# Slot one-hots by 32 f16 tensor-scalar operations that carry the token number

## The reference, cut to what matters

```python
x = x + xattn(layernorm(x), ctx_1024, ...)        # 2 x 1024 tokens of 256, 16 heads, 64 keys
xf = layernorm(x).reshape(2048, 256)
scores = softmax(xf @ gate_w.T)                   # 8 experts
_, sel = top_k(scores + expert_bias, 2)           # 2 experts of each token
order = argsort(sel.reshape(-1), stable=True)     # (token, choice) pairs sorted by expert
token_idx = order // 2
routed = xf[token_idx] * top_scores_sorted
routed_out = grouped_ffn(routed, w1, w2, w3, counts)   # h = silu(x w1[e]) * (x w3[e]); h w2[e]
out = zeros.at[token_idx].add(routed_out)
x = x + out
```

## Time and profile before

| | us |
|---|---|
| three timed runs | 415.96, 419.43, 426.19 (median 419.43) |
| the profiled execution | 411.13 |
| its span, first to last instruction | 409.4 |
| attention and loads (about) | 0 to 149 |
| routing after the prefix matmuls | 149 to 162 |
| experts and the copy out | 162 to 409 |
| busy: TensorE, DVE, ACT, POOL | 358.7, 239.3, 197.4, 234.8 |

### The profile page before, as it was taken

One profiled execution on the slowest core, in us unless ns is written; L12 is line 12 of the kernel. 1 busy time (PEld: TensorE's weight loads), 2 busy tenths in 40 slices (PEclk: granted clock), 3 DMA queues, 4 the chain that ended last, 5 costly groups with the idle time before them and its releaser, 6 DMA issues.

```text
span 409.4 us, 10006 instructions
## 1 busy us (share of the span) xinstructions
PE 358.7 (88%) x2668; PEld 263.6 (64%) x2669; DVE 239.3 (58%) x615; ACT 197.4 (48%) x343; POOL 234.8 (57%) x288
## 2 busy tenths in 40 slices
PE   2767999999999894889999999999999999999810
PEld 2546888888787552457667776677777677776510
DVE  1887767777673578275555555656555656555400
ACT  4577989889887420243343443343443343443200
POOL 7448978887788801224546655556656556663330
PEclk9896999999999996999999999999999999999985
DMA  7944979978977010357677777777777778888636
GB/s 226 355 77 113 254 201 240 243 214 217 253 226 239 31 20 2 78 124 128 130 129 132 138 141 138 129 136 127 143 141 138 128 137 128 142 139 125 98 37 215
DMA packets 121524, 61.55 MB, mean 150 GB/s; under 512 B 97170, under 2 KB 116124, under 8 KB 121468
## 3 DMA queue, kind: packets, MB, share of 16 engines
q1 hardware_dynamic: 113408, 50.45, 51.6%
q0 software_dynamic: 7488, 10.39, 17.2%
q10 hardware_dynamic: 604, 0.41, 0.6%
HBM read 28.88 MB, written 11.60 MB: 99 GB/s over the span
## 4 chain that ended last, share of the span: by engine, by line
PE 74%; DVE 8%; DMA 6%; issue 4%; ACT 3%; POOL 2%; POOLq 0%; SPq 0%; ACTq 0%; DVEq 0%
PE sc L1419 12%; PE sc L1421 11%; PE sc L1420 11%; PE bank L1307 7%; PE bank L1435 6%; PE bank L1438 6%; PE bank L1437 5%; PE bank L1355 3%; PE ptps L1369 3%; DMA acc<-xn,put_now 3%; DMA w_hi<-n_L_xattn_in_proj_weight 2%; PE bank L1322 2%; POOL w_lo L516 1%; PE sc L1244 1%; PE sc L1275 1%
## 5 line engine op out<-in xcount | busy, mean ns | idle before, releaser
L608 POOL DMA_INDIRECT acc<-xn,put_now x39 | 62.3, 1597 | 74.3 <-DVE xn L1149 68.5
L1419 PE MATMUL sc<-w_hi,arena 128*128 x312 | 97.8, 314 | 4.2 <-DMA arena<-x 2.2
L808 ACT ACTIVATE arena<-sc,slot_score 128x352 f32<-128x352 f32 x78 | 43.1, 553 | 115.9 <-PE sc L1421 114.8
L1421 PE MATMUL sc<-w_lo,arena 128*128 x312 | 97.6, 313 | 0.0
L1420 PE MATMUL sc<-w_hi,arena 128*128 x312 | 97.5, 313 | 0.0
L1136 DVE SCALAR_TENSOR_TENSOR arena<-sc,slot_score,arena 128x352 f32<-128x352 f32 x78 | 45.5, 584 | 84.3 <-ACT arena L808 84.3
L516 POOL TENSOR_TENSOR w_lo<-stage_w,w_hi 128x1408 f16<-128x1408 f32 (+1 forms) x32 | 71.7, 2255 | 13.4 <-ACT w_hi L635 12.3
L1435 PE MATMUL bank<-w_hi,arena 128*128 x234 | 63.8, 273 | 3.1 <-DVE xn L1149 1.8
L1438 PE MATMUL bank<-w_lo,arena 128*128 x234 | 61.7, 273 | 0.0
L1437 PE MATMUL bank<-w_hi,arena 128*128 x195 | 53.2, 273 | 0.0
L578 POOL DMA_INDIRECT arena<-table,get_now x32 | 34.4, 1075 | 25.6 <-POOL get_now L572 25.6
(11 more groups left out here) (190 smaller groups left out, 615.5 us busy)
## 6 DMA issues: line engine op xcount, KB each, us to landing
stage_w<-in_L_ffn_w SPq DMA_DIRECT2D x16, 704.0 KB, 4.9
stage_w<-in_L_ffn_w SPq DMA_DIRECT2D x8, 384.0 KB, 4.0
stage_w<-in_L_ffn_w SPq DMA_DIRECT2D x8, 256.0 KB, 4.3
acc<-arena SPq DMA_DIRECT2D x16, 128.0 KB, 2.7
table<-xn SPq DMA_DIRECT2D x16, 128.0 KB, 2.6
arena<-in_x SPq DMA_DIRECT2D x2, 768.0 KB, 8.2
stage_w<-in_L_ffn_w SPq DMA_DIRECT2D x16, 64.0 KB, 4.1
arena<-arena SPq DMA_TRANSPOSE x53, 5.2
```

Source lines behind the costliest of these rows:

```text
L608: pool.indirect_dma_start(out=acc[:, :], out_offset=bass.IndirectOffsetOnAxis(ap=put_now[par][:, 0:1], axis=0), in_=y_sb[par], in_offset=N ...
L808: act.activation(sil[par].rearrange("p (c n) -> p c n", c=2)[:, c, :], h1_ps[:, c, :], ACT.Silu, scale=slot_score[par][:, 0:1]).then_inc(s ...
L1419: pe.matmul(ps[:, c, :], gT[par][:, k, :], w_hi[:, cols], start=k == 0, stop=False)
L1421: ins = pe.matmul(ps[:, c, :], gT[par][:, k, :], w_lo[:, cols], start=False, stop=k == KD - 1)
```

## The change: one operation per one-hot, in f16

Three edits. The tile one-hots are written in f16 and not multiplied any more; the two f32 operations become one, without a wait behind it. The offset one-hots are built by 32 tensor-scalar operations, one per n: (index row == offset) * token number, both scalars per partition, index row and result in f16. Each counts `oneh_ready` up by one, and TensorE waits for it before each of its 32 matmuls. The index row in f16, `iota16`, is a copy of `iota_p` that DVE makes in step 17, between lines 941 and 1033, with a wait for its own end.

```diff
-        oneh_a = take(T * TOPK * J).rearrange("p (n j) -> p n j", j=J)
-        val_a = take(T * TOPK * (J + 1), F16).rearrange("p (n j) -> p n j", j=J + 1)
+        oneh_a = take(T * TOPK * (J + 1), F16).rearrange("p (n j) -> p n j", j=J + 1)
...
+        iota16 = sb("iota16", [P, P], F16)
...
                 if t == T + 1:
                     gate_shift(0, EARLY)
+                    dve.wait_ge(s["consts"], N_CONST)
+                    rlink(dve.tensor_copy(iota16[:, :], iota_p[:, :]))
...
-            def one_hot_b(i):
-
-                nn = slice(i * NP // 2, (i + 1) * NP // 2)
-                dve.tensor_tensor(oneh_b[:, nn, :], iota_p[:, None, :].broadcast_to([P, NP // 2, P]),
-                                  pb[:, nn, None].broadcast_to([P, NP // 2, P]), ALU.is_equal).then_inc(s["oneh_ready"], 1)
-
-            rlink(dve.tensor_tensor(oneh_a, iota_p[:, None, 0:J].broadcast_to([P, NP, J]),
-                                    pa[:, :, None].broadcast_to([P, NP, J]), ALU.is_equal))
-            dve.tensor_tensor(val_a[:, :, 0:J].rearrange("p (t k) j -> p t k j", k=TOPK),
-                              oneh_a.rearrange("p (t k) j -> p t k j", k=TOPK),
-                              tok_id[:, :, None, None].broadcast_to([P, T, TOPK, J]), ALU.mult)\
-                .then_inc(s["oneh_ready"], 1)
-            one_hot_b(0)
-            one_hot_b(1)
+            dve.tensor_tensor(oneh_a[:, :, 0:J], iota_p[:, None, 0:J].broadcast_to([P, NP, J]),
+                              pa[:, :, None].broadcast_to([P, NP, J]), ALU.is_equal).then_inc(s["oneh_ready"], 1)
+            for n in range(NP):
+                dve.tensor_scalar(oneh_b[:, n, :], iota16[:, :], pb[:, n:n + 1], tok_id[:, n // TOPK:n // TOPK + 1],
+                                  ALU.is_equal, ALU.mult).then_inc(s["oneh_ready"], 1)
...
             for n in range(T * TOPK):
-                if n % T == 0:
-                    pe.wait_ge(s["oneh_ready"], 2 + n // T)
-                ins = pe.matmul(bk7[:, 64:64 + J], oneh_b[:, n, :], val_a[:, n, 0:J], start=n == 0,
+                pe.wait_ge(s["oneh_ready"], 2 + n)
+                ins = pe.matmul(bk7[:, 64:64 + J], oneh_b[:, n, :], oneh_a[:, n, 0:J], start=n == 0,
                                 stop=n == T * TOPK - 1)
```

## The result

Twenty runs of each kernel: medians 415.52 us before and 416.79 after, ratio 1.0068 with a 95% interval of 1.0036 to 1.0100. By the ratio the change makes the kernel slower by 0.7%, 2.8 us of 415.5 (1.5 to 4.2). That is under 2%, but clear of no change.

A forecast was written before the change was run, and what follows sets the result against it. DVE alone bounds the one-hot stage, each microsecond moving the gather and all experts. Stage +0.5 and held copy +1.75 give +2.3 us on the 419.43 median: 421.7, range 415.5 to 427.

The forecast's parts named there:

- the sum: Whole change: 0.5 us for the one-hot stage plus 1.75 us for the copy, 2.3 us slower.
- The copy: Step 17 on DVE: the cast is held until POOL's last line 516 ends, so line 1033 starts 1.75 us later.
- 1.3 later: POOL's scale for the last tile (line 540) would wait for line 1041, from 140.88 to 142.05 at the latest.
- DVE, not POOL, would be last: Last logits: ready at 146.1 after POOL's late scale, DVE there at 146.72, so the full 1.75 us reaches the routing.
- TensorE's tail: After the one-hots: one matmul waits instead of 16, but no gain, since lines 1095 and 1097 hold DVE until 161.07.
- The clock: Rival, chance 0.10: TensorE's granted clock halves, slowing the 14 matmuls of line 1244; 1.0 to 2.6 us on top, time 423.5.
- the longer gap before the last tile's transposes: TensorE's idle time there, 0.56 us today, would be 1.9 and might let the granted clock halve.
- the term of the 32 operations: One-hot stage on DVE: 32 operations of 0.20 us make 6.4, stage 7.87 instead of 7.35, 0.5 us longer.
- the 66 of the row with the PSUM source: Column cost of one operation, 66 ns for 128 f16 columns, taken from line 879 at 0.51 ns a column.
- the upper end: One-hot stage if the second scalar costs its own 60 ns: 0.26 us per operation, stage 9.79, 2.4 us longer.
- this is no change: Verdict on the whole kernel: 2.3 us lies under the 2%, 8.4 us, that measurement can tell; same 0.93, slower 0.05.
- The level 421.7: Forecast time in us: 2.3 added to 419.43, the median of three timed runs of the kernel before.

The follow-up runs named there:

- copy_late: Changed kernel with its f16 copy moved behind line 1055, into DVE's wait for the prefix matmuls; ratio to the kernel before 1.0008 (0.9975 to 1.0041), interval 26.01 us.
- copy_x3: Changed kernel with the f16 copy made three times in a row at its old place; logits copy of tile 13 to first gather 28.82 and 28.69 us, against 27.72.
- gap_filled: Changed kernel with three copies plus 12 TensorE filler matmuls; first try, in step 17, missed the gap (interval 26.16 us), second, in step 18, filled it (28.36).
- tail_new: Changed kernel with the copy late, and lines 1095 and 1097 moved behind the gather and scatter indices; interval 25.38 us, against 26.01 without the move.
- copy_only: Kernel before with only the unused f16 copy added in step 17; ratio 1.0025 (0.9986 to 1.0063), interval 26.78 us against 24.75.
- f32_row: Changed kernel with the copy late, its 32 operations reading the f32 index row instead of the f16 copy; 32 in 8.20 us, interval 27.07 us.

## Why the prediction was right, and where it was wrong

**Right: the mechanism, both places and the sign of the sum.** The sum was +2.3 us, the runs give +2.8 and the interval +2.97.

*The copy*, "1.75 us later": measured 1.70, with a cast of 1.65 that ends just behind POOL's last piece, as forecast from line 1005. `copy_late`, `copy_x3` and `gap_filled` show that it was POOL's piece. The Trainium skill (SBUF — State Buffer, section "Who interferes with whom") has the rule: whoever issues first keeps the shared port pair for the whole instruction, and the other is blocked. The trace agrees: 1.65 against 0.23. The delay of POOL's scale, "1.3 later", is 142.05 - 140.88 = 1.17 by its own numbers; it measured 1.23, and DVE came last either way. That DVE, not POOL, would be last at the last logits held in after; in the executions where the clock fell it did not.

*TensorE's tail*, "looks like a gain but is none": right, and `tail_new` shows the price of the two lines that hide it.

*The clock*, a rival of 0.10: the mechanism exists, but not where I put it. I expected the longer gap before the last tile's transposes; it was 0.69 us in after. The gap that matters, 2.60 us, lies in front of the gate matmuls of tile 14, which also wait for the x2 addition of the last tile. I overlooked that wait. Its price, 0.3 us in `copy_only` and 0.6 in `copy_x3`, was also less than the 1.0 to 2.6 that I gave.

**Wrong: the term of the 32 operations, and the reading of the sum.** "So one operation is 154 + 66 + 60 = 280 ns, and 0.20 us in a queue" was mis-sized: 304 ns and 0.223. Two errors with opposite signs made it. The columns cost 184 - 154 = 30 ns, not the 66 of the row with the PSUM source; `f32_row` against the f16 row shows 30 ns saved (337 - 304 = 33 by the lengths). By the Trainium skill (VectorE: DVE Perf Modes, section "The perf-mode tier table (the rule you actually need)") 128 columns in f16 take 33 ns less than in f32, an estimate from four elements a cycle against two. The trace agrees; I had set the table aside because no row had such an operation. And the second scalar, which I took into the upper end only, costs a full 60 ns. 32 x 0.023 = 0.7 us: the stage came out at +1.24, not +0.5.

"Measurement of this kernel tells about 2%, 8.4 us, from no change: this is no change" was the step that made the forecast no change. With 20 runs of each kernel the interval is 0.3% to either side, and a loss of 0.7% is clear of it. The sum itself said slower; I let the spread of three runs overrule it. The level 421.7 also came from those three: their median, 419.43, lay 3.9 above that of twenty, and so the measured 416.79 lies in the range only near its lower end.

## What to carry to other kernels

A per-partition scalar costs a VectorE instruction a fixed time (60 ns here, each), and so does the instruction itself (0.10 us in a queue with 128 columns of f16 and two constants, 0.03 of it the columns); cutting one operation of 2048 columns into 16 of 128 pays only if the faster format saves more than that, which here it did not. Before a copy or cast is put into a gap of VectorE, look at what GpSimd runs at that moment: the same instruction cost 1.65 us in one place and nothing in another, some 9 us later. And read a change of a few microseconds by an interval between two events that both kernels share, not by the span, where the spread of executions was larger than the change.

## What the runs showed of the hardware

DVE holds POOL up as well. In after POOL's line 546, one column, took 1.17 us and ended as DVE's line 959 (two SBUF inputs, 896 columns) ended, although its recorded start is 0.02 us ahead of that line's; in before it began 0.49 us into line 959, took 0.73, and ended 0.13 behind it. In `copy_x3`, where it came 0.14 us before that line, it took 0.27:

```profile
145.55 1.17 POOL L546 TENSOR_SCALAR nmr<-mv,rs 128x1 f32<-128x1 f32 x1
```

```profile
145.57 1.09 DVE L959 TENSOR_TENSOR arena<-arena 128x896 f32<-128x896 f32 x1
```

```profile
143.07 0.27 POOL L546 TENSOR_SCALAR nmr<-mv,rs 128x1 f32<-128x1 f32 x1
143.21 1.09 DVE L959 TENSOR_TENSOR arena<-arena 128x896 f32<-128x896 f32 x1
```

That fits the earlier case of line 941 against line 516, with the parts exchanged.

And the granted clock of the attention steps, ahead of everything that was edited, differs between executions of this kernel: 1.00 over the last steps in before, 0.83 in after, and 0.63 from 120 to 152.5 in `tail_new`, where the logits copy of tile 13 came at 152.52 instead of 137.69. The whole spread of the times shown, 411 to 430 us, is of that size. What starts it was not tried.
